# Six query and key tiles as f32r parts, destination rows five chunks at a time, one store per batch: a one-core graph network kernel

## The reference, cut to what matters

```
h = jnp.maximum(_layernorm(x, axis=-1), 0.0)
q = (x @ Wq + bq).reshape(N, H, HEAD)         # x is h here
k = (x @ Wk + bk).reshape(N, H, HEAD)
adj = jnp.zeros((N, N), jnp.float32).at[edge_index[0], edge_index[1]].set(1.0)
scores = jnp.where(adj[:, None, :] == 0, -1000000000.0, scores)
...
w = jnp.einsum('rb,bio->rio', att, basis)      # relational layer, 30 bases
```

## Time and profile before

| | us |
|---|---|
| median of 3 runs (463.43 to 468.84) | 464.56 |
| the profiled execution's own time | 463.99 |
| its span | 462.2 |
| PE busy in the span | 442.4 |
| DVE busy | 340.3 |
| ACT busy | 241.0 |

### The profile page before, as it was taken

The page is one execution under the profiler, slowest core; times in us unless marked ns, Lnnn a source line. Parts: engine busy times, 40 slices in busy tenths (PEclk is TensorE's granted clock), DMA queues, the critical chain, the costliest instruction groups (busy, mean ns, idle before and its releaser), DMA issues.

```text
span 462.2 us, 6176 instructions
## 1 busy us (share of the span) xinstructions
PE 442.4 (96%) x2202; PEld 273.4 (59%) x2202; DVE 340.3 (74%) x725; ACT 241.0 (52%) x421; POOL 38.4 (8%) x59
## 2 busy tenths in 40 slices
PE   5999999899899999999999999999599999999996
PEld 3434434344343334878776866676267688888885
DVE  3897876899999969879779657675758785866212
ACT  3998784586798634663335436445542533511210
POOL 3330000012311200010010000100000000000000
PEclk8899999999999999999999999999889999999999
DMA  7997535123999999856099766772990740000002
GB/s 261 417 365 170 198 116 211 61 92 142 357 397 403 379 386 384 328 164 246 0 358 423 292 238 255 279 251 71 401 340 26 296 150 34 1 0 2 0 3 91
DMA packets 18906, 99.23 MB, mean 215 GB/s; under 512 B 3903, under 2 KB 4287, under 8 KB 8383
## 3 DMA queue, kind: packets, MB, share of 16 engines
q1 hardware_dynamic: 14151, 72.86, 42.2%
q0 software_dynamic: 4000, 25.18, 14.8%
q10 hardware_dynamic: 720, 0.73, 0.5%
HBM read 93.50 MB, written 5.25 MB: 214 GB/s over the span
## 4 chain that ended last, share of the span: by engine, by line
PE 82%; DMA 10%; DVE 6%; issue 1%; ACT 1%; DVEq 0%; SPq 0%; ACTq 0%
PE bank L1270 18%; PE sbank L1592 9%; DMA bring<-in_basis 9%; PE sbank L1256 8%; PE bank L1343 7%; PE sbank L1326 6%; PE bank L1605 6%; PE bank L1498 5%; PE bank L1577 5%; PE bank L1256 3%; PE bank L1310 3%; PE sbank L1236 3%; PE sbank L1310 3%; PE sbank L1381 2%; PE bank L1404 2%; PE sbank L1458 2%
## 5 line engine op out<-in xcount | busy, mean ns | idle before, releaser
L1256 PE MATMUL sbank<-bring,attw 120*32 120x512 f32 x320 | 40.3, 612 | 4.9 <-DMA bring<-in_basis 4.9
L762 DVE TENSOR_SCALAR cnt<-iota_row,edge_f 128x512 bf16<-128x512 f16 x132 | 40.8, 345 | 4.4 <-PE sbank L1326 4.4
L509 ACT ACTIVATE adjT<-distance,edge_w,edge_f 128x128 bf16<-128x128 bf16 x61 | 29.2, 480 | 2.0 <-PE sbank L1326 2.0
L1326 PE MATMUL sbank<-cnt,adjT 128*128 128x512 bf16 x132 | 30.0, 380 | 0.0
L419 ACT ACTIVATE stat<-stat,eps 128x1 f32<-128x1 f32 x32 | 9.4, 295 | 39.0 <-DVE stat L772 39.0
L1343 PE MATMUL bank<-hT,wring 128*128 128x512 f32 x64 | 28.9, 594 | 0.0
L1185 DVE SCALAR_TENSOR_TENSOR y_lo<-sbank,gate,y_hi 128x512 fp32r<-128x512 f32 x16 | 11.8, 749 | 22.6 <-ACT y_hi L690 22.6
L448 ACT ACTIVATE s<-bank,colsb 128x512 f32<-128x512 f32 x24 | 16.4, 687 | 21.8 <-PE bank L1270 21.8
L1256 PE MATMUL bank<-bring,attw 120*32 120x512 f32 x192 | 23.7, 600 | 2.6 <-DMA bring<-in_basis 2.5
L759 DVE TENSOR_SCALAR adjT<-iota_row,edge_f,edge_w 128x128 bf16<-128x128 f16 x71 | 22.1, 311 | 5.4 <-PE sbank L1326 5.4
L480 ACT ACTIVATE distance<-iota_row,edge_f 128x128 bf16<-128x128 f16 x61 | 24.3, 400 | 1.7
(11 more groups left out here) (227 smaller groups left out, 1062.8 us busy)
## 6 DMA issues: line engine op xcount, KB each, us to landing
bring<-in_basis SPq DMA_DIRECT2D x63, 1024.0 KB, 8.2
wring<-in_weights POOLq DMA_DIRECT2D x8, 1024.0 KB, 10.0
landing<-in_weights POOLq DMA_DIRECT2D x4, 1024.0 KB, 7.2
w_scratch<-stage SPq DMA_DIRECT2D x64, 64.0 KB, 8.0
hT<-in_weights POOLq DMA_DIRECT2D x4, 1024.0 KB, 10.4
qkw<-w_scratch POOLq DMA_DIRECT2D x2, 2048.0 KB, 8.1
rring<-in_rows POOLq DMA_DIRECT2D x12, 256.0 KB, 8.6
hT<-w_scratch POOLq DMA_DIRECT2D x4, 256.0 KB, 6.9
```

What stands on the lines that cost most here:

```text
L509: act.activation(hot_d[:, n % HOT, :], distance[:, i % 2, :], ACT.Relu, scale=minus_w[:, n:n + 1], bias=weight_f[:, n:n + 1]).then_inc(sem ...
L762: dve.tensor_scalar(hot_s[:, n % HOT, :], iota[:, :], src_f[:, n:n + 1], None, ALU.is_equal).then_inc(sem("hot_ready"), 1)
L1256: mm = pe.matmul(unit_bank(b)[32 * j:32 * j + 32, :], attw[0:KB, u // UNITS, g, :], bring[0:KB, u % BATCH, j, :], start=(g == 0), stop=(g ...
L1326: pe.matmul(bank[7][:, :], hot_d[:, n % HOT, :], hot_s[:, n % HOT, :], start=(n == 0), stop=(n == ECH - 1)).then_inc(sem("hot_used"), 1)
```

## The change

Six edits come together.

1. PE makes the first q tile before the first count, and only the first two q tiles in plain f32 (`WHOLE_TILES`). The other two of q and the four of k are made as parts. For that ACT rounds twelve 128x512 pieces (four of `hT`, of Wq and of Wk) in the chunks of `HIGH_AT`, and DVE subtracts twelve times in the chunks of `LOW_AT`. The load of f1a waits for the last k tile now, since the parts of `hT` lie where it lands.
2. `hot_d` becomes zeros and ones. DVE makes it for the first five of eight chunks with one tensor_tensor (`GROUP`, `OWN_HOTS`; for all eight of the first group), ACT for the other three, 45 in all. The weight goes into `hot_s`, whose tensor_scalar now compares and multiplies, with two per-partition scalars.
3. The first norm is regrouped: the square root's table is loaded ahead, roots and relus go in pairs, DVE takes two of the four turned chunks, PE turns into four banks and runs 23 matmuls on zeros ahead.
4. A batch is stored with one transfer of 128 partitions, issued ahead of load n and not behind it. Its destination is seen as 4 x 32 x 512.
5. Between the second convolution and the graph convolution, two units, the turns, four units, two matmuls on zeros, a unit, three matmuls on zeros.
6. Some semaphores are merged.

The core of the diff:

```diff
+WHOLE_TILES = 2
+HIGH_AT = (12, 14, 16, 18, 20, 22, 24, 26, 34, 40, 46, 52)
+LOW_AT = (13, 15, 17, 19, 21, 23, 25, 27, 37, 43, 49, 55)
+GROUP, OWN_HOTS = 8, 5
 def act_hots(n):
-    return n * 15 // 32
+    return max(0, n // GROUP - 1) * (GROUP - OWN_HOTS) + (max(0, n % GROUP - OWN_HOTS) if n >= GROUP else 0)
+def own_hots(n):
+    return min(ECH - n, OWN_HOTS if n else GROUP)
...
-LAST_READ = {"f1a": ("q_psum", C), "f1b": ("v_psum", C), "f2a": ("weight_parts", C),
+LAST_READ = {"f1a": ("k_psum", C), "f1b": ("v_psum", C), "f2a": ("weight_parts", C),
...
                 for n in range(2 * UNITS + 2 * BATCH):
+                    if n % BATCH == BATCH - 1 and n >= 3 * BATCH - 1:
...
+                        sp.dma_start(scratch[layer].rearrange("(j u) q o -> j u q o", j=COLT)[
+                            :, g * BATCH:(g + 1) * BATCH, :, :].rearrange("j g q o -> j (g q) o"),
+                            stage[:, b % SLOTS, :]).then_inc(
+                                sem(f"w_stored{b % SLOTS}"), 16)
                     if n < 2 * UNITS:
...
-                        for j in range(COLT):
-                            at = j * UNITS + g * BATCH
-                            sp.dma_start(scratch[layer, at:at + BATCH, :, :].rearrange("g q o -> (g q) o"),
-                                         stage[32 * j:32 * j + 32, b % SLOTS, :]).then_inc(
-                                             sem(f"w_stored{b % SLOTS}"), 16)
...
+                act.activation(root_of_eps[:, :], eps[:, :], ACT.Sqrt)
...
+                root(0, 0)
+                root(0, 1)
+                relu0(0)
+                relu0(1)
+                root(0, 2)
+                root(0, 3)
+                relu0(2)
+                relu0(3)
+                for c in (2, 3):
+                    turn("hT0", hT, c, 0, C)
+                def qk_high(i):
+                    what, k = divmod(i, C)
+                    if what == 0:
+                        act.wait_ge(sem("hT0"), C)
+                        act.copy(h0_hi[:, k, :], hT[:, k, :]).then_inc(sem("qk_hi"), 1)
+                    else:
+                        name = "qk"[what - 1]
+                        need_weight(act, name)
+                        if name == "k":
+                            act.wait_ge(sem("q_psum"), WHOLE_TILES)
+                            act.wait_ge(sem("qk_parts"), 2 * C)
+                        act.copy(qk_parts[name][0][:, k, :], weight(name)[:, k, :]).then_inc(sem("qk_hi"), 1)
...
                         act.activation(hot_d[:, n % HOT, :], distance[:, i % 2, :], ACT.Relu,
-                                       scale=minus_w[:, n:n + 1], bias=weight_f[:, n:n + 1]).then_inc(
-                                           sem("act_hot_ready"), 1)
+                                       scale=-1.0, bias=ones[:, :]).then_inc(sem("act_hot_ready"), 1)
+                    if n in HIGH_AT:
+                        qk_high(HIGH_AT.index(n))
...
-                    if not on_act(n):
-                        dve.tensor_scalar(hot_d[:, n % HOT, :], iota[:, 0:P], dst_lo[:, n:n + 1],
-                                          weight_f[:, n:n + 1], ALU.is_equal, ALU.mult).then_inc(
-                                              sem("hot_ready"), 1)
-                    dve.tensor_scalar(hot_s[:, n % HOT, :], iota[:, :], src_f[:, n:n + 1], None,
-                                      ALU.is_equal).then_inc(sem("hot_ready"), 1)
+                    if n % GROUP == 0:
+                        m = own_hots(n)
+                        if n >= HOT:
+                            dve.wait_ge(sem("hot_used"), n + m - HOT)
+                        dve.tensor_tensor(hot_d[:, n % HOT:n % HOT + m, :],
+                                          iota[:, 0:P].unsqueeze(1).to_broadcast([P, m, P]),
+                                          dst_lo[:, n:n + m].unsqueeze(2).to_broadcast([P, m, P]),
+                                          ALU.is_equal).then_inc(sem("hot_ready"), 1)
+                    dve.tensor_scalar(hot_s[:, n % HOT, :], iota[:, :], src_f[:, n:n + 1], weight_f[:, n:n + 1],
+                                      ALU.is_equal, ALU.mult).then_inc(sem("hot_ready"), 1)
+                    if n in LOW_AT:
+                        qk_low(LOW_AT.index(n))
...
+                    dve.tensor_tensor(lo[:, k, :], whole[:, k, :], hi[:, k, :].bitcast(F32),
+                                      ALU.subtract).then_inc(sem("qk_parts"), 1)
...
+                for c in (0, 1):
+                    dve.wait_ge(sem("hT0_psum"), c + 1)
+                    dve.tensor_copy(hT[:, :, blk(P, c)],
+                                    bank[c][:, :].rearrange("p (f n) -> p f n", f=C)).then_inc(sem("hT0"), 1)
...
-                dve.tensor_scalar(minus_w[:, :], weight_f, -1.0, None, ALU.mult).then_inc(sem("edge_step"), 1)
...
+                    if which < 2 and t >= WHOLE_TILES:
+                        pe.wait_ge(sem("qk_parts"), (which + 2) * C)
+                        for k in range(C):
+                            mm = parts_tile((h0_hi, h0_lo), qk_parts["qk"[which]], c, k, True)
+                        mm.then_inc(sem("qkv"[which] + "_psum"), 1)
+                        return
...
-                keep_clock(12)
+                keep_clock(23)
                 pe.wait_ge(sem("ident"), 2)
-                for c in range(C):
-                    turn(hr, c, "h0", "hT0")
-                    keep_clock(2)
+                for c, idle in enumerate((0, 4, 1, 2)):
+                    turn(hr, c, "h0", "hT0", base=0, banks=C)
+                    keep_clock(idle)
+                pe.wait_ge(sem("hT0"), C)
+                qkv_tile(0)
...
                 parts_stage("c2_1", x_parts, "c1_1", "c2_1_psum")
-                units(4)
+                units(2)
...
-                units(3)
+                units(4)
+                keep_clock(2, bank[4])
+                units(1)
+                keep_clock(3, bank[4])
```

More of the change, by code:

```diff
@@ L180, in build @@
         cnt_r = (w0_hi, w0_lo)
-        softmax_tmp, edge_i, dst_part, edge_f, edge_w, _, root_hi, root_lo = places(
-            [("softmax_tmp", [P, C, N // 2], F32), ("edge_i", [P, 3, ECH], I32),
-             ("dst_part", [P, 2, ECH], I32), ("edge_f", [P, 5, ECH], F32), ("edge_w", [P, ECH], I32),
+        edge_i, dst_part, edge_f, edge_w, softmax_tmp, _, _, h0_lo, _, root_hi, root_lo = places(
+            [("edge_i", [P, 3, ECH], I32), ("dst_part", [P, 2, ECH], I32), ("edge_f", [P, 5, ECH], F32),
+             ("edge_w", [P, ECH], I32), ("softmax_tmp", [P, C, N // 2], F32),
              ("unused", [P, 2 * C * D - C * N // 2 - 11 * ECH], F32)],
+            [("edges", [P, EDGE_ROOM], F32), ("h0_lo", [P, C, D], F32R),
+             ("unused3", [P, C * D - EDGE_ROOM], F32)],
             [("root_hi", [P, C, D], F32R), ("root_lo", [P, C, D], F32R)])
         x_hi, x_lo = root_hi, root_lo
+        h0_hi = y1_lo
+        qk_parts = {"q": (y0_hi, y0_lo), "k": (w0_hi, w0_lo)}
         ff1_hi, ff1_lo = (root_hi, root_lo), (y0_hi, y0_lo)
         Y_parts = ((y0_hi, y0_lo), (y1_hi, y1_lo))
-        src_f, dst_lo, rel1, field, minus_w = (edge_f[:, a, :] for a in range(5))
+        src_f, dst_lo, rel1, field = (edge_f[:, a, :] for a in range(4))
         weight_f = edge_w[:, :].bitcast(F32)
@@ L234, in stored @@
         def stored(slot, groups):
-            return sum(b % SLOTS == slot for b in range(groups)) * COLT * 16
+            return sum(b % SLOTS == slot for b in range(groups)) * 16
         def weight_parts(name):
@@ L488, in _, with relu0 @@
                     act.dma_start(edge_i[:, i, :], e).then_inc(sem("edges_loaded"), 16)
-                act.wait_ge(sem("eps"), 1)
-                for c in range(C):
-                    root(0, c)
+                act.wait_ge(sem("small"), 1)
+                act.activation(root_of_eps[:, :], eps[:, :], ACT.Sqrt)
+                def relu0(c):
                     act.wait_ge(sem("nbias0"), c + 1)
@@ L757, in one_hots, with qk_low @@
                         dve.wait_ge(sem("hot_used"), n - HOT + 1)
-                    if not on_act(n):
-                        dve.tensor_scalar(hot_d[:, n % HOT, :], iota[:, 0:P], dst_lo[:, n:n + 1],
-                                          weight_f[:, n:n + 1], ALU.is_equal, ALU.mult).then_inc(
-                                              sem("hot_ready"), 1)
-                    dve.tensor_scalar(hot_s[:, n % HOT, :], iota[:, :], src_f[:, n:n + 1], None,
-                                      ALU.is_equal).then_inc(sem("hot_ready"), 1)
+                    if n % GROUP == 0:
[10 more added lines that the diff above has]
+                        qk_low(LOW_AT.index(n))
+                def qk_low(i):
+                    what, k = divmod(i, C)
+                    dve.wait_ge(sem("qk_hi"), i + 1)
+                    if what == 0:
+                        whole, hi, lo = hT, h0_hi, h0_lo
+                    else:
```

(30 more changed lines are left out.)

31 lines of the change are left out of this document (15 added, 16 removed).

## The result

The changed kernel takes 478.22 us (four runs, 474.02 to 478.81) against 464.78 before (four runs): 1.0255 times, 95% interval 1.0168 to 1.0341. It is slower by 13.4 us where 1.5 to 2 less was forecast. Its profiled execution took 478.46, with a span of 476.7.

The account below looks back on a forecast made before the run. PE was taken as the bound (busy 96% of the span), with DVE becoming a second bound in counting. Counting's 1.5 us and 0 for the rest gave 463.99 - 1.5 + 0 = 462.5 us, range 458 to 472.5.

Parts of the forecast that it names:

- Stores: ... I give it nothing: Attention's batch stores: merging four issues into one saves SP 1.5 us, but its loads wait anyway, so counted as 0.
- Rival A: Batch stores: the merged store is carried by four DMA engines, not 16, costing 9.5 us, total 472.0; chance 0.27.
- first term: Rival A's cost in attention, 112 to 182 us: 11 us of extra DMA time in six batches, 7.5 counted.
- second term: Rival A's cost at the loads of 320 to 335 us: 2 us more.
- counting stage: Counting, 15.2 to 80.0 us before: forecast to end at 78.5, a gain of 1.5 us.
- The start: Start of counting: first destination rows forecast at 11.95 us instead of 14.56, bounds 11 and 13.3.
- the walk: Counting, chunk by chunk: PE waits for DVE through chunk 63, then PE is bound; tile 5 at 55, end 78.5.
- Rivals B and D: Counting's source rows: B, second scalar free, 459.2 us, chance 0.10; D, two scalars at half pace, 475 us, chance 0.03.
- upper bound for the source row: DVE in counting: a two-scalar source row at half pace would take 0.425 us; 0.325 was taken.
- what counting saves is passed on whole: Attention: DVE, DMA and PE are level, so time saved in counting reaches the total whole, with nothing more won.
- stretch between the convolutions: Reordered units and dummies there: PE's last gap stays some 2.4 us, clock still falls, effect 0 (bounds -2.1, +1.5).
- Rival C: Between the convolutions: extra units and dummies hold the clock at full, 2.1 us come back, total 460.4; chance 0.13.

Follow-up runs that it names:

- e3: Changed kernel, its store still one transfer but to one contiguous block of 128 x 512 (plain rows), basis rows reordered: 463.22 us, 0.9970 of the kernel before.
- e1: Changed kernel with each batch stored by four transfers of 32 partitions again, still ahead of load n: 464.39 us, 1.0006 of the kernel before.
- e5: Changed kernel with its merged store put back behind load n: 472.97 us, 1.0175 of the kernel before.
- e6: e3 with source rows made with one scalar, the edge weight left out of the counts: 460.34 us, 0.9911 of the kernel before.
- e10: e9 with parts for the four k tiles only, the four q tiles plain: 461.11 us, 0.9927 of the kernel before.
- e7: e3 with the twelve subtractions of the q and k parts moved to GpSimd: 471.12 us, 1.0173 of the kernel before.
- e8: e3 with the order of units between the convolutions as in the kernel before (four units, turns, three units, no dummies): 463.35 us, 0.9974.
- e9: e3 with the gap between the convolutions filled: three units, 13 matmuls on zeros, a unit, 5 on zeros, a unit: 461.16 us, 0.9932.
- e11: e9 with all eight q and k tiles plain, no roundings or subtractions: 461.71 us, 0.9948 of the kernel before.
- e4: Changed kernel with each batch stored by two transfers of 64 partitions, each with outermost dimension 2: 494.16 us, 1.0643 of the kernel before.

## Why the prediction was wrong

The step that failed is "Stores: ... I give it nothing". The merged store, with a destination that begins with a dimension of 4, cost 15.0 us (e3 against the changed kernel; 13.8 by e1). All other edits together gained 1.0 with plain rows (e3 against before) and nothing with four stores (e1), where 1.5 was forecast. Rival A named the mechanism, at a chance of 0.27, and I gave it less than the forecast because no row showed a transfer held to a few engines. But no row could: every transfer that SP or ACT issued in that trace had 16 completions, so its silence was no evidence. The page "DMA: Bandwidth & Descriptors" of the Trainium skill, by its rule on the outermost dimension in the section "Why a DMA increments its semaphore by 16 and not by 1", sided with rival A. The trace agrees: 16, four and two late increments, at 463, 478 and 494 us.

Rival A's own size was 9.5 and should have been 15. Its first term was 7.5 for attention, and the first tile of f1a came 7.9 later. That the two agree is in part luck. PE's waits for the basis on this bank grew by 5.2 us (7.7 for 2.5), and the clock, which rival A left out, made up the rest: it was at half for 10 us between 137 and 178, and never in that stretch before the change. Its second term was 2 for the loads of 320 to 335 (2.3 by the chains). What it left out is the stretch of 214 to 262, +4.4: I had looked at the order of store and load only for what SP's issue costs, and not for what lands behind the store. e5 prices the place at about 5.

The counting stage was forecast at 78.5 and came at 79.7, and at 79.2 with plain rows: -0.3 to -0.8 for -1.5. The start, which I put at 11.95, was 12.47 in the changed kernel but 12.02 with plain rows, so it explains only the difference between these two. The 0.7 that is missing in both is lost in the first half, where DVE is the bound: with plain rows tile 5 begins at 55.65 for 55, and the walk is right from there on. Source rows at 0.323 apart, destination rows at 0.82 long, PE idle on DVE only up to the middle (4.6 us, nine times) are as the walk had them, and e6 confirms it from the other side (-3.0). Rivals B and D are out. (The upper bound for the source row was mis-summed: half the pace with two scalars is 0.07 + 0.12 + 0.27 = 0.46 us, not 0.425, so rival D would have cost 18 us of DVE and not 13.) That what counting saves is passed on whole held for e6 (3.0 and 2.9) and not for e10, where 1.9 us of counting left no mark in the time. GpSimd is no way round DVE (e7).

The stretch between the convolutions was forecast at 0, since the clock would fall still: it fell (0.72 and 0.50 in the windows of plain rows), and e8 gives 0.1. Rival C's price was right too, once the gap was really filled (e9). No run takes the later load of f1a or ACT's copies by themselves; outside the store no run shows a loss.

Grouping five destination rows was weighed against the cost of an instruction in the Trainium skill's page "VectorE: DVE Perf Modes", section "The TRN2 errata — SBUF-src ops pay a fixed extra latency per instruction". For the grouped instruction page and trace agreed, 0.73 us from start to start, and it came so. What tells them apart is the scalar, for which that cost has no term: a second one took a source row from 0.2625 to 0.323, and e6, which drops it, gave 3.0 us back. So the reading of the trace, 0.06 us a scalar and 0.07 a start, is the one that fits. No run has single destination rows beside the rest of the change.

The best version run is the changed kernel with plain rows and a filled gap (e9, or e10 with k parts alone): 461.1 to 461.2, 0.7% under the kernel before and 17 us under the changed one.

## What to carry to other kernels

Before merging transfers, look at the outermost dimension: a merge that turns 32 rows into 4 x 32 narrows the transfer from 16 engines to four, and where the engines are full the wide loads beside it pay for it. The runs show this for the destination; none narrowed the source alone. Put the rows in an order that makes the destination contiguous, and the merge is free. When a trace holds nothing of a shape that the change introduces, that is a gap in the evidence, and the mechanism's price times its chance belongs in the forecast.

An edit that frees the bound engine must be walked against the next bound chunk by chunk: six cheaper tiles were worth 3.9 us on PE and lost the stage 0.7 (e11), for they loaded DVE just where PE already waited for it.

## What the runs showed of the hardware

A store issued by SP, with a destination whose outermost dimension is 4, leaves four late completions on its semaphore and one at its issue; with 2 it leaves two and one, with 32 or 128 rows 16. While loads keep the engines full, such a store slows them: 389, 361 and 319 GB/s in the same stretch.

DVE's source rows, a one-tensor instruction at the fourfold pace, began 0.32 us apart alone and 1.28 apart beside GpSimd's subtractions on two tensors, one for each subtraction. The Trainium skill's page "SBUF — State Buffer", section "Who interferes with whom", speaks of a port pair that the two share and that one holds for a whole instruction. That the two engines take turns, one instruction each, agrees with that.

A gap of PE can cost more than its length. In the changed kernel PE had five gaps of 2.0 to 3.6 us at basis units, and the unit behind each took 1.93 or 1.94 us for 1.00. It isn't so behind every such gap: in e4 the unit behind a wait of 2.95 us at 140.80 took 1.06. Filling the gap between the convolutions with 18 matmuls on zeros (4.2 us of PE that had nothing to do) kept the clock at full there and gave 2.1 us back by the medians, on plain rows.
